# Chunk slots of a two-pass gated recurrence: keys, state weights and the first state transposed by DMA instead of by TensorE and VectorE

## What is computed

```
xn = layernorm(x)
q, k, v = silu(xn Wq'), silu(xn Wk'), silu(xn Wv')        4 heads of 256
f = log_sigmoid(xn Wf') / 8 ;  s = 1 - exp(f) ;  g = exp(f)
pass 1, per token:  S1 = S1 * g + k s'  ;  ok = q S1       S1 is 256 x 256 per head
qv = softmax(ok)
pass 2, per token:  S2 = g * S2 + s v'  ;  ov = qv S2
mixer = (silu(ov) normed by its rms, times g_w) Wo'
ffn = bitlinear(silu(bitlinear(xn, w_gate)) * bitlinear(xn, w_up), w_down)    inner 4096
out = x + mixer + ffn
```

## Time and profile before

| what | value |
|---|---|
| time, median of 3 runs | 1719.47 us (1719.46 to 1722.08) |
| the profiled execution's own time | 1725.29 us |
| its span (core 2, the slowest; the cores from 1698.7 to 1723.7) | 1723.7 us |
| TensorE busy | 1442.7 us, 84% |
| VectorE busy | 1003.5 us, 58% |
| ScalarE busy | 559.6 us, 32% |
| GpSimd busy | 203.6 us, 12% |
| DMA queue of SP | 120080 packets, 180.39 MB, 36.3% of 16 engines |
| mean granted TensorE clock of core 2 | 0.937 |

### The profile page before, as it was taken

The page is one execution under the profiler, slowest core; times in us unless marked ns, Lnnn a source line. Parts: engine busy times, 40 slices in busy tenths (PEclk is TensorE's granted clock), DMA queues, the critical chain, the costliest instruction groups (busy, mean ns, idle before and its releaser), DMA issues.

```text
span 1723.7 us, 25092 instructions; the slowest of 8 cores (1698.7 to 1723.7 us)
## 1 busy us (share of the span) xinstructions
PE 1442.7 (84%) x8440; PEld 749.4 (43%) x8508; DVE 1003.5 (58%) x1635; ACT 559.6 (32%) x986; POOL 203.6 (12%) x225
## 2 busy tenths in 40 slices
PE   3677989687788777777777999999999999999998
PEld 1333434454455444444444444444444444444443
DVE  3454455388865577888884455444455555444553
ACT  2563223444477744444452211111111111111111
POOL 1000000011221111111121111001111111001110
PEclk9888999889999999899998999999999999999999
DMA  8997887155556666655536411110101111101100
GB/s 160 218 206 199 234 235 222 53 162 174 169 168 184 187 174 173 183 168 175 162 102 213 154 43 44 43 34 35 43 25 37 43 44 43 44 25 43 44 25 19
DMA packets 126110, 202.97 MB, mean 118 GB/s; under 512 B 58272, under 2 KB 78752, under 8 KB 124832
## 3 DMA queue, kind: packets, MB, share of 16 engines
q1 hardware_dynamic: 120080, 180.39, 36.3%
q0 software_dynamic: 5904, 20.97, 5.3%
HBM read 167.78 MB, written 29.36 MB: 114 GB/s over the span
## 4 chain that ended last, share of the span: by engine, by line
PE 48%; DMA 19%; DVE 19%; issue 7%; ACT 4%; SPq 1%; POOL 1%; DVEq 1%; ACTq 0%; POOLq 0%
PE ps L263 45%; DMA stg<-wuT 5%; DMA stg<-wgT 5%; DMA stg<-wdT 3%; PE ps L268 3%; DVE STf L297 3%; DVE stI L287 2%; DMA xin<-xp 2%; DVE q L287 2%; DVE part L417 2%; DMA gu_s<-stB 1%; DMA wf<-wfT 1%; DVE stB L454 1%; DMA xin<-xr 1%; DVE b_w L297 1%
## 5 line engine op out<-in xcount | busy, mean ns | idle before, releaser
L263 PE MATMUL ps<-wgu,xnTb 128*128 128x512 fp8e4 x2048 | 469.0, 388 | 3.9 <-DMA xnTb<-xnb 3.9
L263 PEld LDWEIGHTS ps<-wgu,xnTb 128*128 128x128 bf16 x2048 | 203.0, 100 | 252.6 <-issue 31.7
L280 ACT ACTIVATE sg<-ps,ccol 128x512 f32<-128x512 f32 x128 | 87.7, 685 | 518.6 <-PE ps L263 480.2
L263 PE MATMUL ps<-wd,qT 128*128 128x512 fp8e4 x1024 | 223.9, 379 | 0.0
L283 DVE TENSOR_TENSOR gu<-ps,sg 128x512 f32<-128x512 f32 x128 | 88.2, 689 | 160.9 <-PE ps L263 144.4
L263 PEld LDWEIGHTS ps<-wd,qT 128*128 128x128 bf16 x1024 | 100.3, 98 | 120.7 <-issue 0.3
L297 DVE SCALAR_TENSOR_TENSOR ob<-ps,ccol,xa 128x512 f32<-128x512 f32 x32 | 24.0, 751 | 184.9 <-PE ps L263 184.9
L417 DVE TENSOR_REDUCE part<-stg 128x1 f32<-128x1024 f32 x64 | 77.7, 1218 | 67.8 <-DMA stg<-wuT 35.2
L283 POOL TENSOR_TENSOR xa<-xa,xin 128x1024 f32<-128x1024 f32 x16 | 37.9, 2370 | 622.6 <-DMA xa<-at_s 622.6
L301 POOL CAST b_s<-STf 128x512 bf16<-128x512 f32 x64 | 47.1, 738 | 499.2 <-DVE STf L297 422.8
L263 PE MATMUL ps<-wf,xnTa 128*128 128x512 bf16 x250 | 68.5, 434 | 35.1 <-DMA wf<-wfT 26.2
(11 more groups left out here) (140 smaller groups left out, 2120.9 us busy)
## 6 DMA issues: line engine op xcount, KB each, us to landing
stg<-wgT SPq DMA_DIRECT2D x64, 512.0 KB, 5.6
stg<-wuT SPq DMA_DIRECT2D x64, 512.0 KB, 5.2
stg<-wdT SPq DMA_DIRECT2D x64, 512.0 KB, 4.8
xin<-xr SPq DMA_DIRECT2D x32, 512.0 KB, 4.9
xin<-xp SPq DMA_DIRECT2D x16, 512.0 KB, 6.1
gu_s<-stB SPq DMA_DIRECT2D x64, 128.0 KB, 3.6
at_s<-b_wo SPq DMA_DIRECT2D x32, 256.0 KB, 2.0
wgu<-gu_s POOLq DMA_DIRECT2D x8, 1024.0 KB, 17.7
```

The costliest lines, as they stand in the source:

```text
L263: return pe(lambda e: e.matmul(out=out, lhsT=lhsT, rhs=rhs, start=start, stop=stop, skip_group_check=True), *toks, mark=mark)
L280: return sc(lambda e: e.activation(out=out, in_=in_, func=func, **kw), *toks)
```

## The change

Keys, state weights and the state of pass 1 are transposed by DMA from SBUF to SBUF. `KT_` is gone. `K_` issues a transpose of its 512 columns behind its Silu, on a slot of its own (`kd0`, `kd1`), into `b_kT`; `stT_`, placed after the second `GS_el` of a step, transposes the whole 1024 columns of `b_st` into `b_stT` (slot `sd`); `s1_tr` issues one transpose of 512 columns per head (slots `sa0` to `sa3`) at the place where it stood. `b_KV` now holds all keys and then all values, so that the keys of a pair of heads are contiguous; `up` and `ok_pe` read with a stride for it.

```diff
-        b_kt = bt("b_kt", 2048, BF16)
+        b_kT = bt("b_kT", 1024, BF16)
+        b_stT = bt("b_stT", 1024, BF16)
...
-        def s1_tr(g, ring):
-
-            bk = ring.take()
+        def s1_tr(g):
+
             for h in (2 * g, 2 * g + 1):
-                for j in range(2):
-                    for m in range(2):
-                        o = (h % 2) * 512 + j * 256 + m * 128
-                        q = h * 512 + m * 256 + j * 128
-                        p = tr(bk.bf[:, o:o + 128], b_s1[:, q:q + 128], s1c_t[h], k2,
-                               bk.freed, mark=(h % 2 == 1 and j == 1 and m == 1))
-            U[("s1r", g)] = p
-            t = cp(dv, S1b[:, g * 1024:(g + 1) * 1024], bk.bf, p, U.get(("s1b", g)))
-            bk.put(t)
-            s1b_t[2 * g] = s1b_t[2 * g + 1] = t
+                hv = slice(h * 512, (h + 1) * 512)
+                s1b_t[h] = dmaT("sa%d" % h, v3(S1b[:, hv], 4), v3(b_s1[:, hv], 4), s1c_t[h],
+                                U.get(("s1b", g)))
+            U[("s1r", g)] = [s1b_t[2 * g], s1b_t[2 * g + 1]]
...
-            t = act(heads(b_KV[:, h * 1024:(h + 1) * 1024], 2, 0), v3(bk.ap, 2), AF.Silu, p,
-                    U.get(("U", h)))
+            t = act(b_KV[:, hsl(h)], bk.ap, AF.Silu, p, U.get(("U", h)), U.get(("kd", h)))
             bk.put(t)
             d["K%d" % h] = t
+            d["kt%d" % h] = dmaT("kd%d" % h, v3(b_kT[:, hsl(h)], 4), v3(b_KV[:, hsl(h)], 4),
+                                 t, U.get("AT"))
+            U[("kd", h)] = d["kt%d" % h]
...
-        def KT_(c, h):
+        def stT_(c):
             d = B[c]
             s = c % 2
...
-            t = cp(dv, b_kt[:, h * 1024:(h + 1) * 1024], bk.bf, p, U.get(("kt", h)))
-            bk.put(t)
-            d["kt%d" % h] = t
+            d["stT"] = dmaT("sd", v3(b_stT, 8), v3(b_st[s], 8), d["st0"], d["st1"],
+                            U.get(("BT", 0)), U.get(("BT", 1)))
+            U[("trs", s)] = d["stT"]
...
-                    p = mm(o, b_QT[:, h * 256 + j * 128:h * 256 + (j + 1) * 128],
-                           S1b[:, h * 512 + j * 256:h * 512 + (j + 1) * 256],
+                    p = mm(v3(o, 2), b_QT[:, h * 256 + j * 128:h * 256 + (j + 1) * 128],
+                           v3(S1b[:, h * 512:(h + 1) * 512], 4)[:, j::2, :],
...
             GS_el(f, 1)
+            stT_(f)
             dc_el(f)
...
-            s1_tr(0, RC)
+            s1_tr(0)
...
-            KT_(f, 0)
-            s1_tr(1, RC)
+            s1_tr(1)
             Q_(f, 1)
             bg(2)
-            KT_(f, 1)
             V_(f, 0)
```

More of the change, by code:

```diff
@@ L137, in build_nc @@
         slots = {}
-        for n in (["x0", "x1", "t0", "t1", "st0", "st1", "st2", "qs0", "qs1",
+        for n in (["x0", "x1", "t0", "t1", "st0", "st1", "st2", "qs0", "qs1", "sa0", "sa1", "sa2", "sa3", "kd0", "kd1", "sd",
                    "a0", "a1", "o0", "o1", "o2", "o3", "y0", "y1", "wd", "gw"]
@@ L811, in V_ @@
             d["proj"] = p
-            t = act(heads(b_KV[:, h * 1024:(h + 1) * 1024], 2, 256), v3(bk.ap, 2), AF.Silu, p,
+            t = act(b_KV[:, 1024 + h * 512:1536 + h * 512], bk.ap, AF.Silu, p,
                     U.get(("U", h)), U.get(("s2b", h)))
@@ L815, in V_ @@
             d["V%d" % h] = t
-        def KT_(c, h):
+        def stT_(c):
             d = B[c]
             s = c % 2
[L820 to L830, removed]
-            t = cp(dv, b_kt[:, h * 1024:(h + 1) * 1024], bk.bf, p, U.get(("kt", h)))
-            bk.put(t)
-            d["kt%d" % h] = t
+            d["stT"] = dmaT("sd", v3(b_stT, 8), v3(b_st[s], 8), d["st0"], d["st1"],
+                            U.get(("BT", 0)), U.get(("BT", 1)))
+            U[("trs", s)] = d["stT"]
         def kt(h, j):
-            o = (h // 2) * 1024 + (h % 2) * 256 + j * 128
-            return b_kt[:, o:o + 128]
+            o = h * 256 + j * 128
+            return b_kT[:, o:o + 128]
         def stT(h, j):
-            o = (h // 2) * 1024 + 512 + (h % 2) * 256 + j * 128
-            return b_kt[:, o:o + 128]
+            o = h * 256 + j * 128
+            return b_stT[:, o:o + 128]
         def AT_(c):
@@ L851, in AT_ @@
                            bk.freed, mark=(h == 3 and j == 1))
+            U["AT"] = p
             t = tt(dv, v3(b_at, 4), v3(bk.ap, 4),
@@ L873, in ok_pe @@
             U[("s1b", g)] = p
-            U[("st", s, g)] = [p, U.get(("trs", s, g))]
+            U[("st", s, g)] = [p, d["stT"]]
             d["okb%d" % g] = bk
@@ L940, in BT_ @@
                            b_qT[:, h * 256 + j * 128:h * 256 + (j + 1) * 128],
-                           j == 0, j == 1, d["qT%d" % g], bk.freed,
+                           j == 0, j == 1, d["qT%d" % g], d["stT"], bk.freed,
                            mark=(hh == 1 and j == 1))
-            U[("kt", g)] = p
+            U[("BT", g)] = p
             t = tt(dv, v3(b_bt[:, g * 256:(g + 1) * 256], 2), v3(bk.ap[:, 0:256], 2),
@@ L961, in ov_pe @@
                            j == 0, False, s2b_t[h], d["qT%d" % g], bk.freed)
-                    p = mm(o, b_KV[:, h * 512 + 256 + vh * 128:h * 512 + 384 + vh * 128],
+                    p = mm(o, b_KV[:, 1024 + h * 256 + vh * 128:1152 + h * 256 + vh * 128],
                            b_bt[:, h * 128:(h + 1) * 128], False, True, d["bt%d" % g],
@@ L984, in up @@
             bk = RC.take()
-            p = mm(bk.ap, b_w[s][:, g * 128:(g + 1) * 128], b_KV[:, h * 512:(h + 1) * 512],
+            p = mm(v3(bk.ap, 2), b_w[s][:, g * 128:(g + 1) * 128],
+                   b_KV.rearrange("p (t h x) -> p t h x", t=2, h=4)[:, :, h, :],
                    True, True, d["w%d" % (h // 2)], d["K%d" % (h // 2)],
@@ L1041, in build_nc @@
         for g in range(2):
-            s1_tr(g, RC)
+            s1_tr(g)
         for h in range(2):
@@ L1047, in build_nc @@
             GS_el(0, h)
+        stT_(0)
         dc_pe(0)
@@ L1053, in build_nc @@
         for h in range(2):
-            KT_(0, h)
             V_(0, h)
```

## The result

The changed kernel takes 1787.06 us (median of 4 runs, 1782.43 to 1855.14) against 1720.78 (4 runs, 1719.46 to 1726.34): 1.037 times as long, 95% interval 1.0344 to 1.0397, about 64 us. The 1855.14 us are a run in a slower state of the chip, which ratios leave out; in the experiments too they are taken from the other runs alone. The profiled execution took 1782.43 us, with a span of 1780.9 on core 6; the eight cores' spans lie between 1766.6 and 1780.9.

What follows compares the result with a forecast made beforehand. The prediction took quantising chunks to be bound by loads in the full DMA queue. +40 us for ten quantising chunks, +8 for three summing and −4 for the last two made +44, so 1763 us, range 1722 to 1840.

Steps and rivals of the forecast that it cites:

- Bound: A quantising chunk ends with its ninth background job, that job with a load, the load with the queue ahead of it.
- +4.0 us per quantising step: Ten quantising chunks: 4.3 us transpose data plus 0.9 us holes minus 1.2 us VectorE copies each, +40 us in all.
- −1.2 us for VectorE's copies: Per quantising chunk, one `b_kt` and one `S1b` copy leave the chain of waits, saving 1.2 us.
- Holes: DMA traffic falling off behind a transpose among loads: 1.75 us for a whole hole, half a hole (0.9 us) taken per chunk.
- As fast as the best loads: Rival: transposes run at some 460 GB/s, 786 KB taking 1.7 us per chunk, so no change, 1722 us; chance 0.06.
- Step 6: The step going over from sums to quantising, counted among the ten quantising chunks at +4.0 us.
- Sums +2.6: Three summing chunks, with a lower DMA share, pay half of 5.2 us: +2.6 us each, +8 in all.
- Last two steps −1.8 each: The loop's last two chunks gain TensorE's time for 32 transposes, 1.8 us each, −4 in all.
- If the loads went away, they would be bare: Waits for `b_kT` and `S1b`, transposes landing after 4.1 to 6.9 us, are covered only while the loads are there.
- What lies before 335 us doesn't change: The stretch ahead of the chunk loop keeps its time; so does what lies behind 919 us.
- Waits on the results: In the chunk, `AT_` needs `b_kT` at about 719 us, `b_at` has six more us of cover; these waits are covered.
- `b_stT` in the idle stretch costs nothing: The 256 KB state-weight transpose, issued at about 703 us into the DMA engines' idle stretch, adds nothing.

Runs made afterwards that it cites:

- b3: Kernel before the change plus four DMA transposes of 128 KB per step in steps 0 to 12 into a tile nobody reads: 1748.19 us, ratio 1.0129.
- e1: Changed kernel with GpSimd's eight feed-forward weight loads also waiting for the last chunk's key and state transposes: 1755.88 us, ratio 1.0214.
- e2: Changed kernel with the loop's transposes of the pass 1 state back on TensorE and VectorE: 1731.59 us, ratio 1.0056.
- b5: Kernel before with the first state transposes behind the first chunk's projections and only the state weights transposed by DMA: 1712.9 us, ratio 0.9929.
- b6: As b5, but the last step's state-weight transpose stands behind the first feed-forward input load: 1718.14 us, ratio 0.9915.
- b1: Kernel before with the first chunk's state transposes moved behind its projections, same instructions: 1714.86 us, ratio 0.9962.
- b4: As b3, but each of the four added transposes covers only 128 columns (32 KB): ratio 1.0112.
- b2: Kernel before plus four plain 128 KB DMA copies per step in steps 0 to 12 into a tile nobody reads: 1729.58 us, ratio 1.0032.
- c1: e1 with the chunk loop's job stores and loads issued from GpSimd instead of SP: 1819.53 us, ratio 1.0504.

## Why the prediction was right, and where it was wrong

Sign and size held: 1763 us was forecast with 1722 to 1840 around it, 1787 measured. Against the kernel before +44 was forecast, about +64 came. That the two lie so near is in part luck. The forecast is +40 for ten quantising steps, +8 for the sums and −4 for the last two, all by the queue of data. Measured are +38 for the ten, +5, and +25 for the last two, with −11 at the start and +4 in the feed-forward part: one term right in size for another reason, and one miss of 29 us that a miss of 11 in part hides.

*Bound: right at its end.* A quantising step ends with jobs, a load and `b_at`, and in the changed kernel TensorE waits 11.3 us for `b_at` before the step at 708 where it was 6.1. But the 16 us ahead of the last load are SP's issues.

```profile
708.82 0.37 PE L264 MATMUL ps<-b_st,b_at 128*128 128x256 bf16 x1 [11.31 <-DVE b_at L284]
```

*+4.0 us per quantising step: right in size (+3.7 and +2.9), wrong in mechanism.* The step that failed is "SP waits 22.3 us of this chunk for VectorE's `stB`, so the time is there". The half-size issue, put between 0.4 and 1.23 us, is at the upper end, 1.19; and SP's idle time lay at other places of its list than the six transposes. Where several stand between a job and its store, the store and the load behind it start up to 6.4 us late. What I had priced instead, 4.3 us of DMA time and 0.9 of holes, was to show in loads that land after 7 us and more; their median is 5.1 us. The DMA time itself did come, and more of it: with b3's four it rose by 4.2 us per step, 1.05 us each where 0.72 was put, and for the most part fitted in beside the rest. Four transposes by themselves cost 1.65 us per step, not half or two thirds of 5.2. The −1.2 us for VectorE's copies can't be seen in the runs: taking the four out of e1 again, with their copies back on VectorE (e2), shortens the loop by 26.9 us, more than the 21.4 that four without any relief cost in b3. That doesn't rule the relief out, as e1's list holds three more transposes.

*Holes: overpriced.* The transposes among loads left them seldom: the landing before a 128 KB transpose and its own lie 0.53 us apart in the median (b3), those of a 32 KB one 0.23. *"As fast as the best loads": out.* The changed kernel's 1 MB of transposes per step took 7.7 us of DMA time, 136 GB/s and not 460.

*Step 6: not seen.* It took +8.7 us where +4.0 stood. For 13.8 us (595.6 to 609.4) every link of its chain is an issue of SP. Why it is hit harder than the other steps wasn't tested.

*Sums +2.6: +1.6.* *Last two steps −1.8 each: wrong.* Step 13, which still has seven jobs, went up by 2.1, and step 14 by 22.9, the latter because the prediction followed SP's list and the loads in it and not the DMAs of GpSimd's list, which the last projection releases. "If the loads went away, they would be bare" was the right question with the wrong case: what came were more loads, from another queue.

*"What lies before 335 us doesn't change": wrong by 11 us.* The 8.89 us wait for GpSimd's casts stood in the trace, ahead of the loop, where I hadn't looked for what the moved instructions had been blocking.

*Waits on the results: right.* `AT_` waits 1.65 us for `b_kT` in the step shown, and `b_at` comes 12 us later. *`b_stT` in the idle stretch costs nothing: right* (b5, b6: 0.5 to 0.8 us gained in the late steps, which the whole times barely tell apart from b1), except in the last step, where it held back another load by its place in the list, 3.6 us.

On the rules weighed: the Trainium skill, "DMA: Bandwidth & Descriptors", Issuing engines are not separate DMA queues, says that the time to initiate a DMA is usually small relative to the DMA itself. For these transposes it isn't: 1.20 us of issue beside 1.05 us of DMA time (b3). By that rule b4, with about b2's DMA time, would cost what b2 costs (1730 us); it took 1739 to 1758. The same section's other half, that DMAs of all engines share the same 16 and interleave, fits c1 and the last step.

## What to carry to other kernels

A DMA that replaces engine work has two prices, its time on the DMA engines and its time in the issuing list, and a list is judged where the new DMA stands and not by its idle total: ask which store or load is queued behind it. Put it where both list and DMA engines are idle (the state weights here), and keep it clear of bulk loads on another queue. And when instructions leave an engine's order, look for what had been waiting behind them: most of that gain may be had by moving them.

## What the runs showed of the hardware that I had not expected

A DMA transpose holds SP almost the same time whatever its width: in the median 1.13 us for 128 columns (b4), 1.20 for 512 (b3), 1.23 for 1024 (`b_stT` of the changed kernel), always 128 rows of bf16. A plain copy of 128 KB from SBUF to SBUF holds it 0.49 (b2). Four such transposes take 4.2 us of all 16 engines, the four copies 1.3. Beside 8 MB of loads from GpSimd's queue a 128 KB transpose landed after 25.5 us, and SP was held 20 us by the issue of the next two; without the loads beside it (e1) it landed after 2.4.
